# A gate in two stages and a convolution block: batches of 12, 8 and 12 images in place of 16 and 16, with work moved between VectorE and GpSimd

## The reference, cut to what matters

```python
def kan_linear(x, grid, base_w, spline_w, scaler):      # cubic B-splines on 12 knots
    bases = b_splines(x, grid)                           # 8 bases for each input
    return silu(x) @ base_w.T + einsum('bik,oik->bo', bases, spline_w * scaler[:, :, None])
...
s = mean(gn(x), axis=(2, 3))                             # 32 x 128
s = silu(kan_linear(s, grid1, base_w1, spline_w1, scaler1))     # 32 x 16
gate = sigmoid(kan_linear(s, grid2, base_w2, spline_w2, scaler2))   # 32 x 128
x = x + gn(x) * gate
...
z = gn(x)
r = relu(conv1x1(z)); r = relu(conv1x1(r)); route = softmax(mean(conv1x1(r)))
s = relu(conv3x3(z)); spatial_route = softmax(mean(conv3x3(s)))
xp = star_scale * relu(z @ w_pw1) ** 2 + star_bias       # 256 channels
xs = irfft2(rfft2(xp) * (route mixed with complex_weights))
x = x + (xp * (spatial_route mixed with spatial_weights) + xs) @ w_pw2
```

## Time and profile before

| what | value |
|---|---|
| median of 3 runs | 268.7 us (268.66 to 271.92) |
| the profiled execution | 268.3 us, span 266.5 us |
| busy in the span | PE 92%, DVE 73%, ACT 60%, POOL 41% |
| first tap of the convolutions | starts at 32.5 us |
| logits of the first half | start at 74.1 us |
| first mixing product of the rounds | 104.0 us |
| mean granted TensorE clock | 0.997 |

### The profile page before, as it was taken

One profiled execution on the slowest core, in us unless ns is written; L12 is line 12 of the kernel. 1 busy time (PEld: TensorE's weight loads), 2 busy tenths in 40 slices (PEclk: granted clock), 3 DMA queues, 4 the chain that ended last, 5 costly groups with the idle time before them and its releaser, 6 DMA issues.

```text
span 266.5 us, 6842 instructions
## 1 busy us (share of the span) xinstructions
PE 245.8 (92%) x2185; PEld 189.2 (71%) x2185; DVE 195.1 (73%) x542; ACT 160.6 (60%) x376; POOL 110.1 (41%) x198
## 2 busy tenths in 40 slices
PE   0678799999999998999999999999999999999993
PEld 0678665454544455786888888998888888888873
DVE  3998999935919534798498997876768768678672
ACT  2024586456764746664658768667576675775741
...
DMA packets 9482, 13.18 MB, mean 49 GB/s; under 512 B 732, under 2 KB 8924, under 8 KB 9332
## 3 DMA queue, kind: packets, MB, share of 16 engines
...
## 4 chain that ended last, share of the span: by engine, by line
PE 66%; DVE 13%; issue 9%; POOL 5%; ACT 3%; DMA 3%; SPq 0%; POOLq 0%; ACTq 0%; DVEq 0%
PE bank L1149 19%; PE bank L1287 9%; PE bank L1297 7%; PE bank L1243 7%; PE bank L1230 5%; PE bank L1304 4%; PE bank L1059 4%; DMA x_all<-in_x 3%; PE bank L1262 2%; PE bank L1159 2%; POOL prod L412 2%; PE bank L1203 2%; PE bank L1089 1%; DVE qt L983 1%; DVE stats L701 1%
## 5 line engine op out<-in xcount | busy, mean ns | idle before, releaser
L411 POOL TENSOR_TENSOR prod<-t_re,t_im 128x256 f32<-128x256 f32 x32 | 23.3, 730 | 58.0 <-DVE t_re L976 57.1
L957 DVE TENSOR_SCALAR xp<-sq_v,later_sb 128x512 f32<-128x512 f32 x32 | 17.6, 550 | 34.5 <-ACT sq_v L573 34.3
L1149 PE MATMUL bank<-z_all,split_h 128*64 128x450 f16 (+2 forms) x320 | 37.4, 374 | 1.3 <-ACT z_all L489 1.3
L1287 PE MATMUL bank<-later_sb,prod 128*128 128x128 f32 x256 | 36.5, 286 | 1.2 <-POOL prod L412 1.1
L421 POOL TENSOR_TENSOR waves<-folded 128x128 f32<-128x128 f32 x31 | 14.1, 456 | 51.3 <-DVE eo L964 51.2
L1287 PEld LDWEIGHTS bank<-later_sb,prod 128*128 128x128 f32 x256 | 31.1, 192 | 5.3 <-POOL prod L412 3.8
L1243 PE MATMUL bank<-later_sb,eo 128*128 128x128 f32 x256 | 34.0, 276 | 0.0
L1297 PE MATMUL bank<-qt,later_sb 128*128 128x256 f32 x128 | 32.9, 380 | 0.0
L603 ACT ACTIVATE folded<-bank,coef 128x128 f32<-128x128 f32 x32 | 11.8, 367 | 34.5 <-PE bank L1304 28.1
L1243 PEld LDWEIGHTS bank<-later_sb,eo 128*128 128x128 f32 x256 | 31.1, 192 | 1.0 <-issue 0.4
L1149 PEld LDWEIGHTS bank<-z_all,split_h 128*64 128x64 f16 x320 | 17.2, 110 | 18.3 <-issue 4.6
...
## 6 DMA issues: line engine op xcount, KB each, us to landing
x_all<-in_x SPq DMA_DIRECT2D x8, 512.0 KB, 9.0
...
later_sb<-in_later SPq DMA_DIRECT2D x1, 918.5 KB, 9.2
sym_all<-in_sym SPq DMA_DIRECT2D x1, 292.5 KB
...
```

The source lines that it names most:

```text
L411: pool.tensor_tensor(prod[:, :, :, 0, :], halved[0][:, :, 0], halved[1][:, :, 1], ALU.subtract).then_inc(prod_ready, 1)
L1149: last = mm(dst[:, :, rows_out, cols_out], w[:, t, :], pixels(z_all[:, b:b + 2, part, :])[:, :, rows_in, cols_in], start=(n == 0 and t in ...
L1287: last = mm(bank[1][:, odd * C:(odd + 1) * C], prod[:, m, odd].rearrange("p a s -> p (a s)"), pw2_t[:, m, :], start=(m == 0), stop=(m == 1))
```

## The change

There are three batches, images 0 to 11, 12 to 19 and 20 to 31, each with its own semaphores and its own chain. The images are loaded in nine pieces, the first four (twelve images) ahead of the early weights. GpSimd makes the knots' differences and scales the first spline weights; VectorE makes all reciprocals in one instruction. The second spline layer lies on all partitions: the first layer's product is written by four column groups of 32, each for a quarter of the images, so that the layer has 3 or 2 columns where it had 16, and four instructions bring its results to 16 partitions. The weight maxima of VectorE stand elsewhere. GpSimd makes the low parts of blocks 1, 2 and 4 (`z_exact`, `z_low`). `second_pointwise` is four quadrant products of 64 rows and 64 columns. TensorE runs other numbers of filler products. At the first round, the pixels of image 0 are turned behind the second waves, and ScalarE's `second_hidden(7)` stands ahead of `spatial_mix(0)`.

```diff
-X_CHUNKS = 8
+X_CHUNKS = ((0, 4), (4, 8), (8, 10), (10, 12), (12, 16), (16, 20), (20, 24), (24, 28), (28, 32))
+FIRST_CHUNKS = 4
 HALF = NB // 2
 NPAIR = HALF // 2
+BATCHES = ((0, 12), (12, 20), (20, NB))
+QUARTERS = P // 32
...
+            for n in range(FIRST_CHUNKS):
+                load(n)
             sp.dma_start(early_sb[:, :], early).then_inc(in_early, 16)
-            for n in range(X_CHUNKS // 2):
-                load(n)
             sp.dma_start(later_sb[:, :], later).then_inc(in_later, 16)
             sp.dma_start(sym_all[:, :], sym).then_inc(in_sym, 16)
-            for n in range(X_CHUNKS // 2, X_CHUNKS):
+            for n in range(FIRST_CHUNKS, len(X_CHUNKS)):
                 load(n)
...
+            def z_exact(it, batch):
+                pool.wait_ge(coef_ready[batch], 1)
+                for k in range(IT):
+                    b = it * IT + k
+                    pool.tensor_scalar(z32_pool[:, k, :], x_all[:, b, :], coef[:, 2, b:b + 1], coef[:, 3, b:b + 1],
+                                       ALU.mult, ALU.add).then_inc(z32_ready, 1)
+            def z_low(it, nth):
+                pool.wait_ge(z32_ready, IT * nth)
+                pool.wait_ge(zh_ready[it], IT)
+                images = slice(it * IT, (it + 1) * IT)
+                pool.tensor_tensor(z_all[:, images, 1, :], z32_pool[:, :, :], z_all[:, images, 0, :], ALU.subtract).then_inc(zl_ready[it], 1)
+            pool.wait_ge(coef_ready[0], 1)
             pool.wait_ge(split_hi, 1)
             pool.tensor_tensor(split_l[:, :], split_src, split_h[:, :], ALU.subtract).then_inc(split_lo, 1)
-            pool.wait_ge(coef_ready[0], 1)
+            z_exact(1, 0)
+            z_low(1, 1)
+            places(1, 0)
+            pool.wait_ge(zl_ready[1], 1)
+            z_exact(2, 0)
+            places(1, 1)
+            z_low(2, 2)
...
-            places(1, 0)
-            places(1, 1)
+            pool.wait_ge(zl_ready[2], 1)
+            z_exact(4, 1)
+            places(2, 0)
+            z_low(4, 3)
+            places(2, 1)
...
-            z_high(3)
             deviation(1, 1)
+            sigmoid_in(1, 0)
             conv_hidden(0)
+            second_hidden(0)
+            sigmoid_sum(1, 0)
+            sigmoid_in(1, 1)
+            route_hidden(1)
+            conv_hidden(1)
+            sigmoid_sum(1, 1)
+            ahead(ACT.Sqrt)
+            second_hidden(1)
+            deviation(1, 2)
+            act.wait_ge(coef_ready[1], 1)
+            z_high(3, (0, 1))
+            route_hidden(2)
+            z_high(3, (2, 3))
+            conv_hidden(2)
+            second_hidden(2)
+            deviation(2, 1)
+            z_high(4)
             act.wait_ge(filt_done, 2)
             act.activation(filters[:, :], bank[4].bitcast(BF16)[:, 0:512], ACT.Identity).then_inc(filt_ready, 1)
-            second_hidden(0)
-            sigmoid_in(1, 0)
-            route_hidden(1)
-            conv_hidden(1)
-            second_hidden(1)
-            sigmoid_sum(1, 0)
-            sigmoid_in(1, 1)
-            route_hidden(2)
-            conv_hidden(2)
-            second_hidden(2)
-            sigmoid_sum(1, 1)
+            sigmoid_in(2, 0)
+            route_hidden(3)
+            conv_hidden(3)
+            sigmoid_sum(2, 0)
+            sigmoid_in(2, 1)
+            second_hidden(3)
+            sigmoid_sum(2, 1)
             ahead(ACT.Sqrt)
-            route_hidden(3)
-            deviation(1, 2)
-            ahead(ACT.Exp)
-            act.wait_ge(coef_ready[1], 1)
-            z_high(4, (0, 1))
-            conv_hidden(3)
-            second_hidden(3)
-            z_high(5)
             route_hidden(4)
             conv_hidden(4)
+            deviation(2, 2)
+            ahead(ACT.Exp)
             second_hidden(4)
+            act.wait_ge(coef_ready[2], 1)
+            z_high(5, (0, 1))
...
+                    elif layer:
+                        for q in range(QUARTERS):
+                            rows_q = slice(32 * q, 32 * q + KH)
+                            images = slice(images_of(batch).start + q * width, images_of(batch).start + (q + 1) * width)
+                            tt(k_rhs[0:KH, :, images], k_t[rows_q, 0:NK + 1, cols], k_u[rows_q, 0:NK + 1, cols],
+                               ALU.subtract).then_inc(kan_rhs[batch], 1)
...
+            statistics(0, 12)
             channel_stats(0)
             group_spread(0, 1)
-            dve.wait_ge(in_later, 16)
-            for n, span in enumerate(spans):
-                dve.tensor_reduce(maxima[:, n:n + 1], later_sb[:, span], AX, ALU.max, apply_absolute_value=True).then_inc(max_cols, 1)
+            inverses()
+            statistics(12, 13)
             kan_input(0)
             kan_layer(0, 0)
-            dve.wait_ge(max_rows, 1)
-            steps.then(dve.tensor_reduce(maxima_t[:, 0:1], bank[0][0:3, 128:256], AX, ALU.max))
-            dve.tensor_scalar(maxima_d[:, :], ident[0:3, 0:3], maxima_t[:, 0:1], None, ALU.mult).then_inc(max_diag, 1)
+            weight_maxima()
             kan_hidden(0)
-            dve.wait_ge(max_done, 1)
-            steps.then(dve.tensor_scalar(w_max[:, :], bank[0][:, 256:259], 1e-30, None, ALU.max))
-            dve.reciprocal(w_inv[:, :], w_max[:, :]).then_inc(max_ready, 1)
-            kan_layer(0, 1)
-            statistics(HALF, HALF + 4)
+            kan_layer(0, 1, (weight_maximum, lambda: None, weight_scale))
+            statistics(13, 16)
             image_coefficients(0)
-            statistics(HALF + 4, HALF + 6)
+            statistics(16, 17)
             group_spread(0, 2)
-            statistics(HALF + 6, HALF + 9)
+            statistics(17, 19)
             z_coefficients(0)
...
             z_high(0, (2, 3))
+            statistics(19, 20)
+            channel_stats(1)
             z_low(0)
-            statistics(HALF + 9, NB)
-            channel_stats(1)
-            z_low(1)
             group_spread(1, 1)
-            z_low(2)
+            statistics(20, 23)
             kan_input(1)
             kan_layer(1, 0)
-            z_low(3)
+            statistics(23, 26)
             kan_hidden(1)
             kan_layer(1, 1)
+            statistics(26, 29)
             image_coefficients(1)
+            statistics(29, 31)
             group_spread(1, 2)
+            statistics(31, 32)
             z_coefficients(1)
-            z_high(4, (2, 3))
-            z_low(4)
+            channel_stats(2)
+            z_low(3)
+            group_spread(2, 1)
+            kan_input(2)
+            kan_layer(2, 0)
+            kan_hidden(2)
+            kan_layer(2, 1)
+            image_coefficients(2)
             edges(0, 4)
+            group_spread(2, 2)
+            z_coefficients(2)
+            z_high(5, (2, 3))
             windows(0)
...
+            def kan_hidden(batch):
+                width = sizes[batch] // QUARTERS
                 pe.wait_ge(kan_w_ready, 2)
+                pe.wait_ge(hid_zeroed, 2)
...
+                        pe.wait_ge(kan_rhs[batch], 1 + k // NK)
+                    for q in range(QUARTERS):
+                        first = images_of(batch).start + q * width
+                        last = mm(kan_hid[batch][32 * q:32 * q + KH, :], kan1_t[:, k, :], k_rhs[:, k, first:first + width],
+                                  start=(k == 0), stop=(k == NK))
+                last.then_inc(kan_done[batch], 1)
...
             def second_pointwise(it):
                 pe.wait_ge(r1_ready, it + 1)
-                mm(bank[5 + it % 2], rwc_t, r1[:, :], start=True, stop=True).then_inc(rwc_done, 1)
+                if it >= 1:
+                    pe.wait_ge(r2_ready, 2 * it)
+                for g in range(2):
+                    rows_g = slice(HID * g, HID * g + HID)
+                    for k in range(2):
+                        last = mm(bank[5 + g][HID * k:HID * k + HID, 0:HW], rwc_t[rows_g, HID * k:HID * k + HID], r1[rows_g, k * HW:(k + 1) * HW],
+                                  start=True, stop=True)
+                last.then_inc(rwc_done, 1)
             taps(0, 0)
+            group_means(1, 1)
             taps(0, 1)
-            taps(0, 2, 0, 3)
-            group_means(1, 1)
-            taps(0, 2, 3)
+            taps(0, 2, 0, 2)
+            group_variances(1, 1)
+            taps(0, 2, 2)
             second_pointwise(0)
+            taps(1, 0)
+            kan_hidden(1)
+            taps(1, 1)
+            taps(1, 2, 0, 8)
+            kan_sums(1)
+            taps(1, 2, 8)
+            second_pointwise(1)
+            taps(2, 0, 0, 6)
+            group_means(1, 2)
+            taps(2, 0, 6)
+            taps(2, 1, 0, 2)
+            group_variances(1, 2)
+            taps(2, 1, 2)
+            taps(2, 2, 0, 3)
+            group_means(2, 1)
+            taps(2, 2, 3)
+            second_pointwise(2)
             pe.wait_ge(filt_cols, 2 * GROUPS)
+            pe.wait_ge(ident_ready, 1)
             for n in range(4):
```

(42 more changed lines are left out.)

333 lines of the change are left out of this document (183 added, 150 removed).

## The result

The changed kernel takes 284.2 us (283.4 to 284.7, four executions), the kernel before 268.7: a ratio of 1.057, interval 1.053 to 1.060. The profiled execution took 284.2 us in a span of 282.4, against 268.3 before: 15.9 us more. I had forecast 8.1 more.

What follows compares the result with a forecast made beforehand. TensorE was taken to bound the gate-and-convolution stage, the first batch's gate chain the start. Terms -2.2 + 1.25 + 4.9 + 4.4 + 1.6 - 1.85 = +8.1 gave 276.8 us; the forecast's own range was 273.5 to 281.5, the wider one 266.5 to 281.5.

Steps and rivals of the forecast that it cites:

- first batch start: Gate chain of the first batch: convolutions start at 30.3 us, not 32.5, a gain of 2.2 us.
- TensorE's own work: Up to the end of block 4's taps: more short products, less from quadrants and an old wait, together +1.25 us.
- stalls behind GpSimd: GpSimd's low parts hold up VectorE and so TensorE at four places: +4.9 us, bounds 0 and 6.8.
- wait ahead of the logits: TensorE stands before the logits until VectorE's image sums are done: +4.4 us, bounds 3.9 and 4.9.
- clock behind that wait: After the wait before the logits, TensorE starts them at 1.2 GHz: +1.6 us, 0 if the clock holds.
- behind: After the logits: three more quadrant pointwise products save 1.25 us, fewer first-round waits 0.6, together -1.85 us.
- The load: At the start, image 12's load lets VectorE open the spline input at 14.5 us, not 14.67: 0.2 us gained.
- The fillers: In the first gate chain, fewer filler products on TensorE were priced at a loss of 0.1 us.
- The high parts: At the first coefficient product, moving GpSimd's subtraction behind the coefficients was to gain 0.4 us.
- (a) to (d): TensorE waits for block 0's low part, batch 1's first and second layers, batch 2's first: 0.7, 0.6, 1.6, 2.0 us.

Runs made afterwards that it cites:

- Experiment 11: Kernel before with its start's filler products cut to 8, 1, 1, 4, 5 from 8, 2, 4, 8, 16, nothing else: 271.5 us, ratio 1.0085.
- experiment 7: Kernel before with only the second pointwise product as four quadrants, plus the order of the first rounds its banks need: 264.2 us, ratio 0.978.
- experiment 5: Changed kernel with GpSimd's split of the weights held back until the high parts of block 0 are done: 286.9 us, ratio 1.062.
- Experiment 4: Changed kernel with the low parts of blocks 1, 2 and 4 back on VectorE: 278.3 us, ratio 1.035.
- Experiment 3: Changed kernel with the first half's windows and image sums ahead of batch 2's last coefficients on VectorE: 277.9 us, ratio 1.038.
- experiment 8: Changed kernel with image 12 moved back, paced fillers, low parts on VectorE, weight split behind block 0's high parts, image sums before the last coefficients: 275.8 us.
- experiment 10: As experiment 8, but with block 1's low part behind the first group spread of batch 1: 273.3 us, ratio 1.014.
- Experiment 9: Changed kernel with image sums before the last coefficients and low parts on VectorE, block 1's behind batch 1's first group spread: 273.5 us, ratio 1.016.

## Why the forecast was too low

The terms, forecast and measured on the profiled execution. C is the end of block 4's last tap, 84.86 us; "TensorE's own work" is what is left of the stretch from the first tap to C without the stalls and the clock.

| term | forecast | measured |
|---|---|---|
| first batch start | -2.2 | +2.9 |
| TensorE's own work | +1.25 | +1.7 |
| stalls behind GpSimd | +4.9 | +5.6 |
| wait ahead of the logits | +4.4 | +4.4 |
| clock behind that wait | +1.6 | +2.1 |
| clock behind another wait (74 to 78 us) | none | +1.6 |
| behind | -1.85 | -2.4 |
| sum | +8.1 | +15.9 |

**The step that failed is the start**, forecast at -2.2 and measured at +2.9 us: 5.1 of the 7.8 us that the sum was short. With the start as measured and all else as forecast the sum would have been 281.9 us, above the 281.5 at which the range ended. The largest part of the rest is the clock behind the wait at 73.6 us (1.6). Three parts of the start were wrong. The load: I let VectorE open the spline input at 14.5 us; it was 15.84 in the profiled execution (+1.3), about 15.0 in the five experiments that leave image 12 in its place. Moving image 12 gained 1.4 us. The fillers: I took "0.1 for a TensorE that had fewer filler products to do". From the spline input to the coefficients it was 17.1 us where I had 14.6 (+2.5). Up to the end of the second layer it went as forecast (9.6 us, forecast 9.75); all of the loss lies behind it, where VectorE stands 0.87, 1.35 and 0.76 us for results that come late. They come late because fillers at half speed stand in front of ready inputs (the mean was there at 28.10 us, its products began at 29.38), and the short products themselves take up to twice their time. Experiment 11 shows the same with the kernel before: 2.2 us at the first tap from the number of fillers alone, and experiment 7's profiled execution prices half speed under the full number at 3.8. The high parts: I moved the split "behind the coefficients" and counted a gain of 0.4, without asking what VectorE does there. It does the high parts of block 0, and they stand for it: 2.40 us in place of 0.73, so that the first tap comes 2.5 us behind the coefficients and not 1.2 (+1.2; experiment 5 takes the high parts to 0.74). Nor was the 0.4 gained, since VectorE now waits for ScalarE where GpSimd had held it. A stall that is moved has to be priced at its new place.

**GpSimd and VectorE** went as forecast in size and place: 1.26, 0.88, 1.62 and 1.87 us for (a) to (d), against 0.7, 0.6, 1.6 and 2.0. The sum of 5.6 lies within the bounds, but the upper one, 6.8, does not follow from the four places as I priced them: 1.4, 1.0, 1.6 and 2.0 make 6.0. Experiment 4 confirms the cause by taking it away. The Trainium skill, "SBUF — State Buffer", section "Who interferes with whom", also lists tensor_scalar among what can take the shared pair; the 2.40 and 0.74 us of experiment 5 agree, and I had read only its half on two-source instructions.

**Logits and clock.** Forecast at C + 5.45; C is 84.86, the logits start at 90.35, which is C + 5.49, with image sums as the releaser. Experiment 3 takes back 5.3 of the two terms' 6.5 us together.

**The clock elsewhere.** I treated it as a matter of one long wait. It also fell behind a wait of 1.87 us (+1.6: a pass of 3.14 us that takes 2.27, quadrants of 1.13, four products of 0.85), and in other runs behind waits of 1.62 (3.0 us, experiment 5), 2.62 (2.75, experiment 8) and 2.50 us (1.7, experiment 10). Each stall of the forecast had this price as a possible second part, and my range had no room for it. Why the clock falls behind one such wait and not behind an equal one stays open.

**TensorE's own work and the quadrants.** Experiment 9 has little to disturb it. From the first tap to C it is 44.69 us, of which 2.64 are waits; before 40.57 (first tap to the end of the earlier trace rows), of which 0.49: 1.97 more work. Four quadrant products save 1.84 there (0.46 each), so the short products of the third batch cost 3.8, where I had 3.45. The Trainium skill, "TensorEngine Tiling (Array Packing)", section "Key Properties", says that a change of tiling mode drains the engine and gives no price; with my 0.6 us for that it would have been 4.05. The measured 3.8 lies between, and no run shows a drain apart. Experiment 7 gives the quadrants and the order of the first rounds together 4.5 us; the forecast had 0.42 for each of eight and 0.6, which is 4.0.

What stays open: experiments 9 and 10 end 4.6 and 4.4 us above the kernel before (268.9 in the same comparison), and 9 above experiment 7 by 9.3. Of the 9.3, experiment 9's trace gives 3.0 to waits (3.95 up to the logits, against 0.95 in experiment 7), 4.2 to short products (3.8 and a variance behind C) and 2.1 to the later first tap. Whether three batches can be made to pay with another order of VectorE's work was not tried.
